# Last mixture of a decoder kernel: gathers issued in portions, unread matmuls beside the loop, answer rows added before their transposes

## The reference

```python
    xf = x.reshape(-1, C)                          # T = 1792 tokens
    cap = int(CAP_FACTOR * T / E)                  # E = 32 experts, cap = 70
    ...
    probs = jax.nn.softmax(h @ r2_w.T, -1)
    topp, topi = jax.lax.top_k(probs, TOPK)        # TOPK = 2
    ...
    score = jnp.where(routed, probs, -jnp.inf)
    idx = jnp.argsort(-score, axis=0)[:cap].T      # 70 tokens of each expert
    valid = jnp.take_along_axis(routed.T, idx, 1)
    w = jnp.take_along_axis(Wc.T, idx, 1) * valid
    xe = xf[idx]
    up = jnp.einsum('eci,eji->ecj', xe, w_up)
    gate, upv = jnp.split(up, 2, axis=-1)
    hact = jax.nn.silu(gate) * upv
    ye = jnp.einsum('ecj,eoj->eco', hact, w_down)
    out = jnp.zeros((T, C), xf.dtype).at[idx.reshape(-1)].add((w[..., None] * ye).reshape(-1, C))
    ...
    out = out + jnp.einsum('tg,tgo->to', gw, ay)   # 16 adapters, one for each pair of experts
    x = x + mixture(layernorm(x))
```

## Time and profile before

| | us |
|---|---|
| median of 3 runs | 3799.75 |
| lowest, highest | 3795.43, 3820.61 |
| the profiled execution's own time | 3812.16 |
| its span | 3810.4 |
| mean granted TensorE clock | 0.948 of full |

### The profile page before, as it was taken

One profiled execution on the slowest core, in us unless ns is written; L12 is line 12 of the kernel. 1 busy time (PEld: TensorE's weight loads), 2 busy tenths in 40 slices (PEclk: granted clock), 3 DMA queues, 4 the chain that ended last, 5 costly groups with the idle time before them and its releaser, 6 DMA issues. The chain is left out here.

```text
span 3810.4 us, 110666 instructions
## 1 busy us (share of the span) xinstructions
PE 3447.9 (90%) x46768; PEld 2411.7 (63%) x46768; DVE 2381.6 (63%) x4435; ACT 2087.9 (55%) x3581; POOL 1618.1 (42%) x1884
## 2 busy tenths in 40 slices
PE   7986669999999697889999999799999999999878
PEld 5654237777777344657777777343446777777548
DVE  5523568877776354468877776233667877777552
ACT  4333557777777222147777776334446777776511
POOL 1100157677674000047777664000336776776121
PEclk9999979999999798899999999899999999999967
DMA  4054136665664243036666564110015666656423
GB/s 164 2 227 168 47 84 155 153 159 144 154 156 97 51 117 82 4 88 152 149 160 148 149 158 100 47 61 23 13 43 140 156 154 152 159 145 153 123 68 106
DMA packets 206109, 439.22 MB, mean 115 GB/s; under 512 B 88210, under 2 KB 101111, under 8 KB 205448
## 3 DMA queue, kind: packets, MB, share of 16 engines
q1 hardware_dynamic: 202760, 430.07, 42.7%
q0 software_dynamic: 1440, 1.83, 0.2%
q10 hardware_dynamic: 1440, 0.52, 0.1%
HBM read 184.67 MB, written 5.40 MB: 50 GB/s over the span
## 5 line engine op out<-in xcount | busy, mean ns | idle before, releaser
L1562 DVE TENSOR_REDUCE x_bank_top<-ps 112x1 f32<-112x500 f32 x2304 | 1414.2, 672 | 447.8 <-PE ps L1264 440.8
L1410 ACT ACTIVATE x_probs_t<-ps 128x896 f32<-128x896 f32 x768 | 703.3, 916 | 127.6 <-PE ps L1285 122.6
L1264 PE MATMUL ps<-x_keys,x_queries 96*112 96x500 bf16 x2304 | 653.6, 382 | 42.5 <-DMA x_queries<-x_query_part 18.6
L1285 PEld LDWEIGHTS ps<-x_queries,x_keys 128*128 128x128 bf16 x9216 | 509.2, 97 | 245.6 <-issue 139.8
L1285 PE MATMUL ps<-x_queries,x_keys 128*128 128x112 bf16 x9216 | 580.9, 213 | 5.4 <-ACT x_probs_t L1410 4.2
L1299 PE MATMUL ps<-x_probs_t,x_values 128*32 128x112 f32 x18432 | 483.4, 261 | 8.9 <-ACT x_probs_t L1412 8.9
L1299 PEld LDWEIGHTS ps<-x_probs_t,x_values 128*32 128x32 f32 x18432 | 436.9, 110 | 70.1 <-issue 39.4
L1488 POOL TENSOR_TENSOR x_key_part<-x_key_whole,x_nothing 128x500 bf16<-128x500 f32 x270 | 337.3, 1249 | 256.8 <-ACT x_key_whole L1394 256.8
L1412 ACT ACTIVATE x_probs_t<-ps 128x448 f32<-128x448 f32 x768 | 414.5, 540 | 0.0
L1264 PEld LDWEIGHTS ps<-x_keys,x_queries 96*112 96x112 bf16 x2304 | 262.6, 131 | 170.9 <-DVE x_bank_top L1562 69.8
L1496 POOL TENSOR_TENSOR x_key_part<-x_key_left,x_nothing 128x500 bf16<-128x500 f32 x270 | 335.8, 1244 | 14.1
(11 more groups left out here) (510 smaller groups left out, 4332.1 us busy)
## 6 DMA issues: line engine op xcount, KB each, us to landing
x_keys<-x_key_part SPq DMA_DIRECT2D x1152, 192.0 KB, 3.8
x_ctx_t<-in_ctx_t SPq DMA_DIRECT2D x96, 750.0 KB, 6.2
cm_ctx_n<-in_ctx_n SPq DMA_DIRECT2D x32, 768.0 KB, 6.2
cm_ctx_t<-in_ctx_t SPq DMA_DIRECT2D x32, 750.0 KB, 8.6
x_queries<-x_query_part SPq DMA_DIRECT2D x558, 28.0 KB, 2.5
e_share<-m_weight_rows SPq DMA_DIRECT2D x32, 448.0 KB, 6.0
m_w<-in_L_ffn_experts SPq DMA_DIRECT2D x16, 768.0 KB, 5.7
e_share<-m_weight_rows SPq DMA_DIRECT2D x8, 896.0 KB, 5.3
```

Of the source, the lines that this page charges most:

```text
L1264: nc.tensor.matmul(ps[0:RW, n, 0:KB], queries[i // 2 % 2][0:TALL, p, i % 2, :], keys[i % 2][0:TALL, p, KB * n:KB * n + KB], start=True, st ...
L1285: mm = nc.tensor.matmul(ps[:, turned_bank(i, p) + c // VC, RW * (c % VC):RW * (c % VC) + RW], keys[i % 2][:, p, KT * c:KT * c + KT], queri ...
L1410: nc.scalar.activation(goal[:, 0:VR - 1], ps[:, bank:bank + VR - 1, 0:VC * RW], ACT.Exp, scale=scale).then_inc(exp_done, 1)
L1562: nc.vector.tensor_reduce(bank_top[0:RW, p, n:n + 1], ps[0:RW, n, 0:KB], AX_X, ALU.max).then_inc(topped, 1)
```

## The change

Five edits, all in `mixture_3`.

1. POOL issues 8 gathers ahead, then one more for each pair, when that pair's `up` is done, with the scatters of finished tiles between them.
2. The groups become tiles 0 and 1, 2 and 3, then 4 to 7, 8 to 11, 12 to 15, and 16 and 17.
3. `stay_busy(4)` ahead of the gathered tiles becomes `stay_busy(6)`; one unread matmul comes before `up(0)` and one behind it; ten come behind the loop, once all result tiles are weighed.
4. ACT's table for silu is loaded ahead of the first copy of gathered tokens.
5. At the end DVE adds the two rows of each token in `back` (`join`), PE only transposes the sum (4 transposes a chunk in place of 8 matmuls), and DVE adds it to `x`, one chunk behind.

```diff
-    FIRST, GROUP = 2, 4
+    GROUP, AHEAD = 4, 8
+    GROUPS = (0, 2, 4, 8, 12, 16, TILES)
...
     def groups_for(n):
         last = (2 * CAP * (min(n, PAIRS - 1) + 1) - 1) // P
-        return max(last - FIRST, -1) // GROUP + 2
+        return next(g for g in range(len(GROUPS)) if GROUPS[g] > last)

     def tiles_of(g):
-        return range(max(FIRST + GROUP * (g - 1), 0), min(FIRST + GROUP * g, TILES))
+        return range(GROUPS[g], GROUPS[g + 1])
...
-            stay_busy(4)
+            stay_busy(6)
...
             for g in range(groups_for(0)):
                 turn_gathered(g)
+            stay_busy(1)
             up(0)
+            stay_busy(1)
...
-            for c in range(CH):
-                pe.wait_ge(answers_landed[c], 16)
+            pe.wait_ge(s["weighted"], TILES)
+            stay_busy(10)
+            for c in range(CH):
+                pe.wait_ge(s["joined"], c + 1)
                 for t in range(TC):
-                    for k in range(2):
-                        mm = nc.tensor.matmul(ps[:, c, PAIR * t:PAIR * t + PAIR], back[c][:, t, k, :], chip.ident[0:PAIR, 0:PAIR], start=(k == 0), stop=(k == 1))
+                    mm = nc.tensor.transpose(ps[:, c, PAIR * t:PAIR * t + PAIR], back[c][:, t, 0, :], chip.ident[0:PAIR, 0:PAIR])
                 mm.then_inc(s["summed"], 1)
...
+            nc.scalar.preload_act_table_set("silu_and_others")
             for g in range(groups_for(0)):
                 keep_gathered(g)
...
-            for j in range(TILES):
+            def gather(j):
                 nc.gpsimd.indirect_dma_start(gathered[:, j, :], None, table, ...)
-            pool.wait_ge(s["emptied"], 16 * CH)
-            for j in range(TILES):
+
+            def scatter(j):
                 r = slice(0, lines_in(j))
                 pool.wait_ge(s["weighted"], j + 1)
                 nc.gpsimd.indirect_dma_start(answers, ...)
+            for j in range(AHEAD):
+                gather(j)
+            pool.wait_ge(s["emptied"], 16 * CH)
+            for n in range(PAIRS + 1):
+                if AHEAD + n < TILES:
+                    pool.wait_ge(s["up_done"], n + 1)
+                    gather(AHEAD + n)
+                for j in finished(n - 1):
+                    scatter(j)
...
-            for c in range(CH):
+            def join(c):
+                dve.wait_ge(answers_landed[c], 16)
+                nc.vector.tensor_tensor(back[c][:, :, 0, :], back[c][:, :, 0, :], back[c][:, :, 1, :], ALU.add).then_inc(s["joined"], 1)
+
+            def add(c):
                 goal = x[:, CB * c:CB * c + CB, 0:S]
                 dve.wait_ge(s["summed"], c + 1)
                 nc.vector.tensor_tensor(goal, goal, ps[:, c, 0:CT].rearrange("p (b s) -> p b s", s=S), ALU.add).then_inc(s["added"], 1)
+
+            join(0)
+            for c in range(1, CH):
+                join(c)
+                add(c - 1)
+            add(CH - 1)
```

More of the change, by code:

```diff
@@ L1970, in mixture_3 @@
             " gathered_turned gathered_kept up_done gate_kept hidden_ready down_done down_kept result_turned weighted slot_chain slots_ready"
-            " scattered summed added stored")
+            " scattered joined summed added stored")
     s = {k: chip.sem("m3_" + k) for k in sems.split()}
```

## The result

| | before | changed |
|---|---|---|
| median us (20 runs each) | 3798.39 | 3777.61 |
| ratio, 95% interval | | 0.9933 [0.9917, 0.9949] |
| profiled execution: own time, span | 3812.16, 3810.4 | 3778.35, 3776.5 |
| first gather to the end of the span | 3810.4 - 3684.6 = 125.8 | 3776.5 - 3687.3 = 89.2 |

The change is 20.8 us faster at the median, 0.55%, where 33 had been forecast; the ratio puts the gain at 0.7%. A ratio here leaves out executions in the chip's slower state (more than 1.5% above the fastest of the same kernel), a median leaves out none. Within the profiled stage the gain is 36.6 us, where the sum said 36.2.

The account below looks back on a forecast made before the run. PE was taken to bound the expert loop, its first half at half clock. 29.3 - 0.9 + 5.2 - 1.0 + 3.6 = 36.2 us off 3812.2 gave 3776, or 3767 at the median; range 3750 to 3796.

Parts of the forecast that it names:

- Clock in the loop: Expert loop: unread matmuls keep PE at full clock, 29.3 us gained, less 0.9 for those around up(0).
- Smaller groups: First up(1) needs two turned tiles in place of four: 0.4 us at most, left out of the sum.
- The stall: PE's waits on "issue" in the third up (the hole), laid to the long gather row: 5.2 us gained.
- The late gather: Tiles 12 to 15, turned behind up(9): PE may wait for gather 15; 1.0 us lost, bounds 0 to 3.
- The end: Last chunks of back: join and fewer PE instructions gain 3.6 us, or 0 if the ten unread matmuls run at half clock.
- From the profiled execution to the median: Median lay 12.4 us below the profiled execution; the same gain gives 3763.6, moved to 3767 as less may be gained.
- A: Clock stays up but the stall isn't the gathers': 31 us gained, 3772 from 3767; chance 0.17 together with late gathers.
- C: Clock falls and doesn't return in the loop, as four-transpose turns stand at other steps: 22.7 us slower, 3822; chance 0.08.

Follow-up runs that it names:

- e5: The change with stay_busy(4) ahead of the gathered tiles and no unread matmuls around up(0); median 3806.5 us, ratio 1.0004.
- e1: Before with only the new unread matmuls ahead: stay_busy(6) and one on each side of up(0); median 3804.7 us, ratio 1.0011.
- e10: The change with the old groups (tiles 0 and 1, then four each); median 3804.8 us, ratio 1.0000.
- e2: Before with only the gathers in portions and the smaller groups; median 3802.4 us, ratio 1.0000.
- e8: The change with all 18 gathers in one row, stay_busy(4) ahead and no unread matmuls around up(0); median 3795.0 us, ratio 0.9955.
- e4: The change with all 18 gathers in one row again; median 3770.5 us, ratio 0.9928.
- e6: The change without the ten unread matmuls behind the loop; median 3774.0 us, ratio 0.9929.
- e7: The change with ten gathers ahead in place of eight; median 3773.3 us, ratio 0.9928.
- e9: Before with only the new unread matmuls ahead and around up(0) and the smaller groups; median 3779.1 us, ratio 0.9930.
- e11: The change with stay_busy(6) but without the two unread matmuls around up(0); median 3774.5 us, ratio 0.9920.
- e0: The kernel before, unchanged, run and profiled again; median 3796.6 us, ratio 0.9985.
- e3: Before with only the join at the end, no unread matmuls there; median 3797.4 us, ratio 0.9981.

## Why the prediction was right or wrong

**Clock in the loop.** The mechanism was right: PE idled at the first gathered tiles, the clock fell there, and a busy loop did not bring it back for tens of microseconds. e5 shows 99 us of it. The saving in the profiled execution came as summed: up to the last weighing 33.6 us, where 29.3 - 0.9 + 5.2 - 1.0 = 32.6 had been forecast.

**Smaller groups.** This was the wrong step. I had written "0.4 us at most, left out". They are one of the two edits that the main effect needs: with the old groups (e1, e10) the clock falls before the second `up`, with the smaller ones and without the two more unread matmuls (e2, e5, e8) at the first tiles. Only both together keep it in the profiles and at the median (the change, e4, e6, e7, e9, e11). That the clock stayed up as forecast is luck in this point: the change happened to hold the edit that had been put at nothing.

**The stall.** That it would go was right; that the portions take it away was not shown. It was there in the four profiles with old groups and a row of 18 (before, e0, e1, e3), and absent with small groups and a row (e4, e8, e9) and with old groups and portions (e10). So either edit is enough, as far as one profile of each run tells, and in the change the portions do nothing that can be measured (e4). What the stall is stays open: in it, semaphores that PE had to raise reached ACT and SP late.

**The late gather.** Charged 1.0 us, measured 0.60, at the tiles that were named.

**The end.** Charged 3.6 us, measured 3.0. All of it is the join; the ten unread matmuls were weighed as a risk and are neither gain nor loss (e6). They took 7.79 us, where 20 x 0.375 = 7.5 had been summed; the earlier trace rows would have given 20 x 0.41 = 8.2.

**From the profiled execution to the median.** Here the size was missed: 33 us forecast, 20.8 measured. The term is the 29.3 us. The half-clock stretch was 68, 38, 31, 48 and 38 us in five profiles of kernels that lose the clock there (before, e0, e1, e2, e3). In e0, the execution near the median, PE was busy for 33.05 us at half clock and not for 61.4, and 33.05 x 0.48 = 15.9. With that the sum is 15.9 - 0.9 + 5.2 - 1.0 + 3.6 = 22.8 us, and the stages differ by 111.4 - 89.2 = 22.2. I had noted that the median lay 12.4 us below the profile, and took off only some 3. Taking off those 12.4 us whole gives 36.2 - 12.4 = 23.8.

**Rivals.** A, that the stall isn't the gathers', is half true and cost nothing: the row of 18 alone does not make it (e4, e8, e9). Nor is it seen that instructions had to be fetched: in none of the four holes does the DMA view show a transfer of an instruction queue, in the first profile the nearest are at 3696 and 3715. C is nearly what e5 and e8, which keep the smaller groups alone, show in their profiles. C's place was read rightly, see the last section: the clock came back only where gathered tiles were turned.

## What to carry to other kernels

Where TensorE works in a pattern that keeps the clock it enters with for tens of microseconds, look at the last few microseconds ahead of the loop and between its first steps, and shorten or fill the pauses there. Here there were two such places. Either one left as it was gave back the gain at the median, so parts tried one at a time showed nothing, and only the pair did; not every pause had to go (0.55 and 0.75 us stayed in e11). And before a saving read from one profile is promised, ask whether that execution was the usual one: compare its own time with the median, and take the difference off.

## What the runs showed of the hardware that was not expected

At half clock a PE that was busy for 98.33 of 99 us did not get its clock back (e5), and at full clock the same pattern kept it for 64 us (e4, e9). The half-clock stretch differs from one execution to the next by tens of microseconds, but it does not end just anywhere. In all eight profiles in which the clock fell, it rose 0.7 to 2.2 us behind the start of a turn of gathered tiles: four transposes and one of a result at 3756.38 (before), 3725.58 (e0), 3724.08 (e1), 3754.77 (e2), 3733.64 (e3) and 3712.45 (e10), and two and one at 3790.27 (e5) and 3788.43 (e8). In e5:

```profile
3790.27 0.63 PE L2135 MATMUL ps<-ident,m_gathered 128*128 128x128 f32 x2
...
3791.63 0.61 PE L2161 MATMUL ps<-m_hidden,m_w 128*128 128x70 f32 x4
```

The same four matmuls had taken 1.06 us one step earlier. Not every such turn lifted the clock: in e5 those at 3696.60, 3709.18, 3738.51 and 3760.72 did not. That the transposes cause the rise is not shown; no run changes them alone.

Ahead of the loop the same trace has a quick return. Behind a wait of 2.22 us the clock of before is at 0.50 from 3679 to 3682, and under unread matmuls of 448 columns it is whole again by 3683:

```profile
3679.00:3683.00 4.00, 4.00 (x8) 1.83 (x6) 0.22 (x1) 0.00 (x0) 0.00 (x0) 0.57 0.02 4
3683.00:3687.00 4.00, 3.57 (x10) 1.57 (x9) 0.26 (x2) 0.00 (x0) 2.12 (x2) 1.00 0.08 20
```

PE is busy all the time in both stretches, here and in the loop; in one the clock comes back and in the other it does not. Unread matmuls inside the loop, to bring it back, were not tried.

In the hole, ACT waited 13.5 to 14.5 us for an `up` that PE's rows show as done 9 to 10 us earlier (before, e0, e1, e3). In e1 the late copy of its fourth tile, 1.9 us behind the transpose, came before the hole. Nothing in these traces names the cause.
